# A macaron block of mixture-of-experts, linear attention and mixture-of-experts: rows of an expert pair merged by a TensorE product, and two output planes in place of four

## The chip, the cores and the metric

The kernel runs on one core of a Trainium2 chip. The metric is the device time of one execution in microseconds (us); the median of three is given. Five engines take part, each with an instruction queue of its own that is worked off strictly in order: TensorE (PE in the profile; its weight loads are PEld), VectorE (DVE), ScalarE (ACT), GpSimd (POOL) and SyncE (SP, which here only issues transfers). They meet through semaphores: an instruction can wait until a semaphore has reached a number, and everything behind it on its engine waits too.

## What is computed

The input is 8 sequences of 512 tokens of 128 features, so 4096 tokens. Three stages follow each other, each with a layernorm in front and its result added to `x`:

```python
x = x + 0.5 * ffn(layernorm(x))
x = x + linear_attention(layernorm(x))      # 16 heads of 8, causal
x = x + 0.5 * ffn(layernorm(x))

def ffn(x):                                  # E = 64 experts, K = 6, CAP = 64
    scores = softmax(x @ gate_w.T)
    _, idx = top_k(scores + gate_b, 6)       # weights are the unbiased scores
    # the first 64 (token, expert) pairs of an expert, in token order, get a slot
    h = silu(xb @ w1.T) * (xb @ w3.T)        # inner width 88
    yb = h @ w2.T
    y[token] += yb[expert, slot] * weight    # scatter-add over all slots
    z = silu(x @ ws1.T) * (x @ ws3.T) @ ws2.T    # shared expert, inner width 176
    return y + z
```

Both ffn stages use the same weights.

## The kernel before

Each ffn stage (`ffn(f)`, f = 0 and 1) has four parts.

**Routing.** Layernorm, logits, softmax and top 6 over four groups of 1024 tokens. Then the slot lists: `scan`, `differences`, `table`, `look_up` and `slots`, each in four quarters of 16 experts (`h` = 0 to 3), find for every slot its token. The quarters 0 and 1 are done ahead of the slab loop, 2 and 3 inside its first steps. `slots(h)` writes the row indices `tok_i` (for the gather) and `put_i` (for the scatter) of 8 slabs.

**The slab loop.** A slab is a pair of experts, 2 x 64 = 128 slots, one per partition; there are 32. Every engine writes its part as one loop over `s` with a software pipeline over three steps:

- POOL issues `gather(s)`, an indirect DMA (L466) that fetches 128 token rows into `GAT`, ten slabs ahead, and `add(s)` (L452), an indirect DMA that adds the 128 weighed rows `Y[:, s]` to the output planes in HBM. `add(s)` waits for `y_sb` of its slab. The scatter of slab `s` also waits until that of `s - 2` has landed.
- PE, in step `s`: `xb_turn(s)` (L758, a transpose), `hidden(s - 1)` (L769, four products), `expert_out(s - 2)` (L778, two products, the experts' output rows in PSUM), then `shared_part(s)`.
- ACT: `copy_xbT(s)`, `silu(s - 1)` and the silu of the shared layer (L560).
- DVE: `gate(s - 1)` (L1083), `weigh(s - 2)` (L1106 twice, PSUM to `Y`, times gate weight, times 0.5, signals `y_sb`), then its share of `shared_part(s)`.

**The shared expert** is spread over the same loop: for 8 groups of 512 tokens. Groups 6 and 7 have their first layer ahead of the loop. Groups 0 to 5 take four steps each from step 8 on (`s = 8 + 4g + k`): at k = 0 and 1 the first layer of one half (L705 on PE, two products of 512 columns; `shared_gate` on DVE, L1094), at k = 2 the second layer (`shared_out`, L718; `shared_add`, L1099), at k = 3 nothing.

**The output planes.** A token can be met by several slots, and two scatter-adds on one row of HBM must not race. So there are four planes, interleaved by token (`4 * token + plane`); the plane of a row is given by the half of the slab (which of the two experts) and by the slab's parity. The planes are zeroed ahead of use by SP (`clear_planes`, 2 MB each), and at the end of the ffn stage SP loads them back (L345) in four groups of 1024 tokens, into the tiles `A`, `PL`, `Bb` and `Cb`; DVE's `update(g)` adds the four planes of a group to `X` (L957, four instructions of 1024 elements per partition). In the middle of the program the next layernorm follows group by group (`stats` on DVE, `normalise` on ACT, L508); at the end the output store follows (L366).

The attention stage between the two is not touched.

What sets the order is the program text: each engine's instructions stand in the order in which its loop issues them. No scheduler moves them.

## Time and profile before

| | us |
|---|---|
| median of 3 runs (lowest, highest) | 533.45 (532.67, 536.54) |
| the profiled execution: its own time | 532.9 |
| the profiled execution: span, first to last instruction | 531.2 |
| PE, DVE, POOL, ACT busy in the span | 356.6, 307.6, 237.0, 207.8 |
| slab loop of f = 0: first gather to the last scatter's issue | 52.1 to 161.6 |
| slab loop of f = 1: the same | 393.3 to 497.0 |

The span is cut into stages that differ in what limits them, so the busy shares over the whole say little; the sections below go by stage. Times in rows are counted from the span's start. In the timeline a row has its start, its duration, the engine, the line and the operation, and in brackets how long the engine sat idle ahead of it and what ended that.

### The profile page before, as it was taken

Reading aid. Unit: us, or ns where it says so; the run is one execution under the profiler, and the core shown is the slowest. Engines: PE = TensorE matmul, PEld = TensorE weight load, DVE = VectorE, ACT = ScalarE, POOL = GpSimd, SP = SyncE. Lnnn points to the kernel's source line nnn. Section 1 sums busy time; section 2 is a strip of 40 time slices with the busy share of each in tenths; the row PEclk is TensorE's granted clock in tenths of the full one; section 3 lists DMA queues with packets and bytes.
Section 4 is the critical chain, followed back from the end, with each engine's and each line's share of the span. In section 5 each row is a group of like instructions: output and inputs, shape, how many; then the busy total and the mean of one; then the engine's idle time right before and its main releaser. Section 6 shows DMA issues by size and latency. Waiting matters only on the chain.

```text
span 531.2 us, 14693 instructions
## 1 busy us (share of the span) xinstructions
PE 356.6 (67%) x5808; PEld 263.3 (50%) x5812; DVE 307.6 (58%) x999; ACT 207.8 (39%) x543; POOL 237.0 (45%) x215
## 2 busy tenths in 40 slices
PE   0874589999960013598999999218848999998000
PEld 0851475666650012376788888118327667666000
DVE  6488363545430994454777775394985544545077
ACT  3983112322310067744677762169722232231000
POOL 7161747887872000403333333001537888887400
PEclk9987567999995556678999999657855699999555
DMA  8999961001015996000111111454200100100396
GB/s 272 369 268 341 318 185 15 5 11 14 5 6 218 407 401 239 2 2 2 40 40 40 40 40 49 109 218 139 61 8 8 12 11 6 17 5 6 108 426 257
DMA packets 49746, 62.64 MB, mean 118 GB/s; under 512 B 21701, under 2 KB 36248, under 8 KB 47183
## 3 DMA queue, kind: packets, MB, share of 16 engines
q1 hardware_dynamic: 37423, 60.51, 33.3%
q0 software_dynamic: 12288, 1.70, 3.2%
q8 instruction: 17, 0.28, 0.2%
q14 instruction: 18, 0.15, 0.1%
HBM read 39.53 MB, written 31.46 MB: 134 GB/s over the span
## 4 chain that ended last, share of the span: by engine, by line
PE 53%; DVE 23%; DMA 9%; ACT 6%; issue 5%; POOL 3%; SPq 1%; POOLq 0%; DVEq 0%; ACTq 0%
PE bank L769 6%; PE upper L864 5%; PE bank L705 5%; DVE X L957 5%; PE bank L718 5%; PE upper L705 4%; DMA Cb<-planes_d 4%; PE upper L778 3%; DVE Cb L1094 3%; DVE bn L962 3%; DVE Cb L1025 3%; POOL planes_d L452 3%; ACT Cb L560 2%; ACT A L508 2%; PE bank L880 2%
## 5 line engine op out<-in xcount | busy, mean ns | idle before, releaser
L452 POOL DMA_INDIRECT planes_d<-Bb,put_i x64 | 101.4, 1584 | 28.0 <-issue 14.8
L480 POOL TENSOR_TENSOR Bb<-Cb,chm 128x576 f32<-128x576 f32 x32 | 36.9, 1183 | 124.3 <-PE upper L909 69.6
L466 POOL DMA_INDIRECT A<-rows_d,tok_i x64 | 68.0, 1063 | 41.6 <-DVE put_i L1066 22.7
L672 PE MATMUL bank<-ident,A 128*128 128x128 f32 x96 | 21.3, 396 | 81.9 <-ACT A L508 65.1
L672 PEld LDWEIGHTS bank<-ident,A 128*128 128x128 f32 x96 | 17.0, 209 | 85.1 <-ACT A L508 52.3
L1106 DVE TENSOR_SCALAR Bb<-upper,A 64x128 f32<-64x128 f32 x128 | 44.4, 347 | 1.3
L1094 DVE TENSOR_TENSOR Cb<-Cb,upper 88x512 f32<-88x512 f32 x24 | 16.4, 683 | 44.8 <-ACT Cb L560 44.8
L769 PEld LDWEIGHTS bank<-ring,w1s 128*88 128x88 f32 x256 | 34.2, 191 | 8.0 <-issue 8.0
L433 POOL TENSOR_TENSOR Bb<-Eb,st 128x512 f32<-128x512 f32 x8 | 8.3, 1043 | 63.8 <-DVE st L1013 63.8
L560 ACT ACTIVATE Cb<-bank 88x512 f32<-88x512 f32 x24 | 14.2, 592 | 55.1 <-PE upper L705 55.1
L769 PE MATMUL bank<-ring,w3s 128*88 128x64 f32 x256 | 35.6, 270 | 0.0
L705 PE MATMUL bank<-XT,ws1s 128*88 128x512 f32 x56 | 32.1, 656 | 3.7 <-DVE Cb L1094 3.7
L769 PE MATMUL bank<-ring,w1s 128*88 128x64 f32 x256 | 34.1, 264 | 0.0
L1083 DVE TENSOR_TENSOR ring<-ring,bank 88x128 f32<-88x128 f32 x64 | 18.0, 281 | 26.2 <-ACT ring L572 26.1
L778 PE MATMUL upper<-w2s,ring 88*64 88x128 f32 x256 | 31.4, 328 | 0.1
L864 PE MATMUL upper<-A,Bb 32*32 32x128 f32 x1024 | 30.8, 273 | 1.0 <-issue 1.0
L769 PEld LDWEIGHTS bank<-ring,w3s 128*88 128x88 f32 x256 | 30.2, 185 | 0.0
L615 ACT ACTIVATE A<-Bb,hm 128x512 f32<-128x512 f32 x32 | 20.5, 711 | 24.1 <-PE upper L864 22.2
L705 PE MATMUL upper<-XT,ws3s 128*88 128x512 f32 x56 | 29.8, 615 | 0.0
L508 ACT ACTIVATE A<-X,st 128x128 f32<-128x128 f32 x72 | 28.6, 481 | 0.0
L957 DVE TENSOR_TENSOR X<-X,A 128x1024 f32<-128x1024 f32 x8 | 9.8, 1225 | 31.5 <-DMA A<-planes_d 31.3
L718 PE MATMUL bank<-ws2s,Cb 88*128 88x128 f32 x192 | 24.6, 281 | 3.9 <-DVE Cb L1094 3.6
(162 smaller groups left out, 804.7 us busy)
## 6 DMA issues: line engine op xcount, KB each, us to landing
planes_d<-zeros SPq DMA_DIRECT2D x8, 2048.0 KB, 15.9
rows_d<-A SPq DMA_DIRECT2D x8, 512.0 KB, 6.0
A<-planes_d SPq DMA_DIRECT2D x4, 1024.0 KB, 6.0
PL<-planes_d SPq DMA_DIRECT2D x4, 1024.0 KB, 10.0
Bb<-planes_d SPq DMA_DIRECT2D x4, 1024.0 KB, 13.7
Cb<-planes_d SPq DMA_DIRECT2D x4, 1024.0 KB, 18.0
w1s<-in_w1T SPq DMA_DIRECT2D x4, 704.0 KB
w3s<-in_w3T SPq DMA_DIRECT2D x4, 704.0 KB
```

Source lines behind the costliest of these rows:

```text
L452: pool.indirect_dma_start(out=planes_d[f], in_=Y[:, s, :], in_offset=None, out_offset=bass.IndirectOffsetOnAxis(ap=put_i[:, s:s + 1], axis=0),
L466: pool.indirect_dma_start(out=GAT[:, t % RING, :], out_offset=None, in_=rows_d, in_offset=bass.IndirectOffsetOnAxis(ap=tok_i[:, t:t + 1], ...
L480: pool.tensor_tensor(out=VX[:, :, :, c, :].rearrange("p q h f -> p (q h) f"), in0=VN.rearrange("p q h f -> p (q h) f"), in1=chm[:, c:c + 1 ...
L508: ins = act.activation(A[:, i, :], X[:, i, :], ACT.Identity, bias=st[:, 1, i:i + 1], scale=st[:, 4, i:i + 1])
L672: ins = pe.transpose(bank[g % 2][:, (i % 4) * P:(i % 4 + 1) * P], A[:, i, :], ident[:, :])
L705: ins = pe.matmul(bank[bk][0:I, :], w[:, k * I:(k + 1) * I], XT[:, 512 * g:512 * g + 512], start=True, stop=True)
L718: ins = pe.matmul(bank[SHARED[0]][:, i * D:(i + 1) * D], hs(g)[k][:, i * P:(i + 1) * P], ws2s[:, k, :], start=(k == 0), stop=(k == 1))
L769: ins = pe.matmul(bank[2 + s % 2][0:I, cols], w[:, 2 * s + k, :], XBT[s % 2][:, CAP * k:CAP * k + CAP], start=True, stop=True)
L778: ins = pe.matmul(bank[(4, 7)[s % 2]][CAP * k:CAP * k + CAP, 0:D], GT[s % 2][:, CAP * k:CAP * k + CAP], w2s[:, 2 * s + k, :], start=True, ...
L864: ins = pe.matmul(bank[4 + g][CHUNK * c:CHUNK * c + CHUNK, q * P:(q + 1) * P] .rearrange("p (j t) -> p j t", j=4), KT[rows, t0:t0 + CHUNK] ...
L957: then(dve.tensor_tensor(xt, xt, PLANES[g].rearrange("p (i k d) -> p i k d", i=GI, k=4)[:, :, k, :], ALU.add))
L1106: ins = dve.tensor_scalar(Y[rows, s, :], bank[(4, 7)[s % 2]][rows, 0:D], GAT[rows, s % RING, col:col + 1], 0.5, ALU.mult, ALU.mult)
```

## The change

Two output planes remain, one for each parity of the slab: the row is `2 * token + (s mod 2)`. So the two experts of a slab write to the same plane, and a token that both have would be met twice by one scatter. The kernel now merges such rows ahead of the scatter:

- `spread(h)` (DVE) writes for 8 slabs the token numbers of the first expert's 64 slots onto a diagonal (`ROWS`); `token_rows(h)` (PE, a product of ones with 512 columns) turns that into rows that hold those numbers on every partition; `match(h)` (DVE, four instructions) compares them with the second expert's token numbers, which gives 64x64 matrices `SAME` for 8 slabs, and moves the index of a second-half row that has a partner beyond the bounds, so that the scatter drops it.
- `merge(s)` (PE) multiplies `SAME` by the second half of `Y`, and `add_second(s)` (DVE) adds the product to the first half and signals `y_sb`.
- In each loop step PE issues `expert_out(s - 2)` ahead of `hidden(s - 1)`, and `merge(s - 2)` behind it. DVE issues `weigh(s - 2)` ahead of `gate(s - 1)`, and `add_second(s - 2)` behind it. `weigh` signals `weighed` and no longer halves; `update` does that (a multiply-add in place of an add).
- `table(3)` moves on DVE one step ahead, `look_up(3)` on PE one step back. The row turns stand at steps 0, 5, 11 and 19, `spread` ahead of the loop and at 4, 10 and 18, `match` at 1, 6, 11 and 19.
- The zeroing is 4 MB per ffn stage and all of it for f = 0 is issued at the start; the loads at the end of a stage are 4 MB in place of 8, and `update` has two instructions per group in place of four.

```diff
-        planes_d = [nc.dram_tensor(f"planes{f}_d", (4 * T, D), F32, kind="Internal").ap() for f in range(2)]
+        planes_d = [nc.dram_tensor(f"planes{f}_d", (2 * T, D), F32, kind="Internal").ap() for f in range(2)]
...
+        ROWS = Eb[0:CAP, :].rearrange("p (s c) -> p s c", s=NS)
+        SAME = Eb[CAP:P, :].rearrange("p (s c) -> p s c", s=NS)
...
-        PLANES = (A_flat, PL[:, :], Bb[:, 0:T], Cb[:, 0:T])
+        HP = T // 2
+        PLANES = (A_flat[:, 0:HP], A_flat[:, HP:T], PL[:, 0:HP], PL[:, HP:T])
...
-            clear_planes(sp, 0, (0, 1))
+            clear_planes(sp, 0)
...
-                    clear_planes(sp, 0, (2, 3))
                     for h in range(1, NQT):
                         load_experts(h)
...
+                def token_rows(h):
+                    pe.wait_ge(rows_set, NQT * f + h + 1)
+                    if NQT * f + h:
+                        pe.wait_ge(same_ready, NQT * f + h)
+                    ss = slice(QSL * h, QSL * h + QSL)
+                    pe.matmul(bank[LOOK[1]][CAP:P, :], ones[:, :], ROWS[:, ss, :].rearrange("p s c -> p (s c)"),
+                              start=True, stop=True).then_inc(rows_ps, 1)
+
+                def merge(s):
+                    if s % QSL == 0:
+                        pe.wait_ge(same_ready, NQT * f + s // QSL + 1)
+                    pe.wait_ge(weighed, f * NS + s + 1)
+                    pe.matmul(bank[(4, 7)[s % 2]][0:CAP, D:2 * D], SAME[:, s, :], Y[CAP:P, s, :], start=True, stop=True)\
+                        .then_inc(merged, 1)
...
                     if s < NS:
                         xb_turn(s)
+                    if s == 2:
+                        pe.wait_ge(dr_sb, NQT * (f + 1))
+                    if s == 3:
+                        pe.wait_ge(table_ready, NQT * (f + 1))
+                    if s >= 2:
+                        expert_out(s - 2)
                     if 1 <= s <= NS:
                         hidden(s - 1)
-                    if s == 2:
-                        pe.wait_ge(dr_sb, NQT * (f + 1))
                     if s >= 2:
-                        expert_out(s - 2)
+                        merge(s - 2)
+                    if s in ROW_TURN:
+                        token_rows(1 + ROW_TURN.index(s))
...
-                    for k in range(4):
-                        then(dve.tensor_tensor(xt, xt, PLANES[g].rearrange("p (i k d) -> p i k d", i=GI, k=4)[:, :, k, :], ALU.add))
+                    for k in range(2):
+                        then(dve.scalar_tensor_tensor(xt, PLANES[g].rearrange("p (i k d) -> p i k d", i=GI, k=2)[:, :, k, :], 0.5,
+                                                      xt, ALU.mult, ALU.add))
...
+                def spread(h):
+                    ss = slice(QSL * h, QSL * h + QSL)
+                    dve.tensor_tensor(ROWS[:, ss, :], ident[0:CAP, 0:CAP].unsqueeze(1).broadcast_to([CAP, QSL, CAP]),
+                                      sl[0:CAP, 1, ss].unsqueeze(2).broadcast_to([CAP, QSL, CAP]), ALU.mult).then_inc(rows_set, 1)
+
+                def match(h):
+
+                    ss = slice(QSL * h, QSL * h + QSL)
+                    dve.wait_ge(rows_ps, NQT * f + h + 1)
+                    then(dve.tensor_tensor(SAME[:, ss, :], bank[LOOK[1]][CAP:P, :].rearrange("p (s c) -> p s c", s=QSL),
+                                           sl[CAP:P, 1, ss].unsqueeze(2).broadcast_to([CAP, QSL, CAP]), ALU.is_equal))
+                    then(dve.tensor_reduce(sl[CAP:P, 0, ss], SAME[:, ss, :], AX, ALU.max))
+                    then(dve.scalar_tensor_tensor(sl[CAP:P, 0, ss], sl[CAP:P, 0, ss], float(T), sl[CAP:P, 1, ss], ALU.mult, ALU.add))
+                    dve.scalar_tensor_tensor(put_i[CAP:P, ss], sl[CAP:P, 0, ss], 2.0, plane0[CAP:P, ss], ALU.mult, ALU.add)\
+                        .then_inc(same_ready, 1)
...
-                        ins = dve.tensor_scalar(Y[rows, s, :], bank[(4, 7)[s % 2]][rows, 0:D], GAT[rows, s % RING, col:col + 1], 0.5,
-                                                ALU.mult, ALU.mult)
-                    ins.then_inc(y_sb, 1)
+                        ins = dve.tensor_scalar(Y[rows, s, :], bank[(4, 7)[s % 2]][rows, 0:D], GAT[rows, s % RING, col:col + 1], None,
+                                                ALU.mult)
+                    ins.then_inc(weighed, 1)
+
+                def add_second(s):
+                    dve.wait_ge(merged, f * NS + s + 1)
+                    dve.tensor_tensor(Y[0:CAP, s, :], bank[(4, 7)[s % 2]][0:CAP, D:2 * D], Y[0:CAP, s, :], ALU.add).then_inc(y_sb, 1)
 
                 for s in range(NS + 2):
+                    if s >= 2:
+                        weigh(s - 2)
                     if 1 <= s <= NS:
                         gate(s - 1)
+                    if s == 1:
+                        match(0)
                     if s >= 2:
-                        weigh(s - 2)
+                        add_second(s - 2)
                     if s == 1:
                         slots(2)
-                    elif s == 2:
                         table(3)
                     elif s == 3:
                         slots(3)
+                    elif s in SPREAD:
+                        spread(1 + SPREAD.index(s))
+                    elif s in MATCH:
+                        match(1 + MATCH.index(s))
```

How the order on PE changes in the steady part of the loop, from the shared first layer of k = 1 to the second layer of k = 2. Before, `xb_turn` (L758), `hidden` (L769), `expert_out` (L778), then the next shared layer (L718):

```order
L705 MATMUL bank<-XT,ws1s 88x512 [waits sh_gated]
L705 MATMUL upper<-XT,ws3s 88x512
L758 MATMUL bank<-ident,A 128x128 [waits xbT_sb,gathered2]
L769 MATMUL bank<-ring,w1s 88x64 [waits gated,xbT_sb]
L769 MATMUL bank<-ring,w1s 88x64
L769 MATMUL bank<-ring,w3s 88x64 x2
L778 MATMUL upper<-w2s,ring 64x128 [waits y_sb,gated]
L778 MATMUL upper<-w2s,ring 64x128
L718 MATMUL bank<-ws2s,Cb 128x128 [waits sh_gated,tokens_ready]
L718 MATMUL bank<-ws2s,Cb 128x128 x7
```

The same step in the changed kernel (L718 is the shared first layer, L773 the transpose, L808 `expert_out`, L784 `hidden`, L800 `merge`, L731 the second layer):

```order
L718 MATMUL bank<-XT,ws1s 88x512 [waits sh_gated]
L718 MATMUL upper<-XT,ws3s 88x512
L773 MATMUL bank<-ident,A 128x128 [waits xbT_sb,gathered2]
L808 MATMUL upper<-w2s,ring 64x128 [waits y_sb,gated]
L808 MATMUL upper<-w2s,ring 64x128
L784 MATMUL bank<-ring,w1s 88x64 [waits gated,xbT_sb]
L784 MATMUL bank<-ring,w1s 88x64
L784 MATMUL bank<-ring,w3s 88x64 x2
L800 MATMUL upper<-Bb,Eb 64x128 [waits weighed,same_ready]
L731 MATMUL bank<-ws2s,Cb 128x128 [waits sh_gated,tokens_ready]
L731 MATMUL bank<-ws2s,Cb 128x128 x7
```

`expert_out` went ahead of `hidden`, and a product that waits for `weighed` now stands between `hidden` and the next shared layer.

On DVE, the same steps before: L1094 is the shared gate, L1083 `gate`, L1106 `weigh`.

```order
L1094 TENSOR_TENSOR Cb<-Cb,upper 88x512 [waits sh_silu]
L1083 TENSOR_TENSOR ring<-ring,bank 88x128 [waits y_ps,silu_done]
L1106 TENSOR_SCALAR Bb<-upper,A 64x128 [waits y_ps]
L1106 TENSOR_SCALAR Bb<-upper,A 64x128
L1094 TENSOR_TENSOR Cb<-Cb,upper 88x512 [waits sh_silu]
L1083 TENSOR_TENSOR ring<-ring,bank 88x128 [waits y_ps,silu_done]
L1106 TENSOR_SCALAR Bb<-upper,A 64x128 [waits y_ps]
L1106 TENSOR_SCALAR Bb<-upper,A 64x128
```

In the changed kernel (L1149 shared gate, L1161 `weigh`, L1138 `gate`, L1167 `add_second`):

```order
L1149 TENSOR_TENSOR Cb<-Cb,upper 88x512 [waits sh_silu]
L1161 TENSOR_SCALAR Bb<-upper,A 64x128 [waits y_ps]
L1161 TENSOR_SCALAR Bb<-upper,A 64x128
L1138 TENSOR_TENSOR ring<-ring,bank 88x128 [waits y_ps,silu_done]
L1167 TENSOR_TENSOR Bb<-upper,Bb 64x128 [waits merged]
L1149 TENSOR_TENSOR Cb<-Cb,upper 88x512 [waits sh_silu]
L1161 TENSOR_SCALAR Bb<-upper,A 64x128 [waits y_ps]
L1161 TENSOR_SCALAR Bb<-upper,A 64x128
L1138 TENSOR_TENSOR ring<-ring,bank 88x128 [waits y_ps,silu_done]
L1167 TENSOR_TENSOR Bb<-upper,Bb 64x128 [waits merged]
```

`weigh` now stands directly behind the shared gate of the step before, and `add_second` waits for PE. The third place is DVE in step 1 and at the first `weigh`; before: `gate(0)`, `slots(2)` (L1062 to L1066), `gate(1)`, `weigh(0)`.

```order
L1083 TENSOR_TENSOR ring<-ring,bank 88x128 [waits silu_done]
L1062 TENSOR_SCALAR top<-bank,c_of_p 128x256 [waits look_ps]
L1063 TENSOR_REDUCE sl<-top 128x8 [waits dve_step]
L1064 TENSOR_TENSOR sl<-sl,bank 128x8 [waits dve_step]
L1065 CAST tok_i<-sl 128x8 [waits dve_step]
L1066 SCALAR_TENSOR_TENSOR put_i<-sl,plane 128x8
L1083 TENSOR_TENSOR ring<-ring,bank 88x128 [waits silu_done]
L1106 TENSOR_SCALAR Bb<-upper,A 64x128 [waits y_ps]
L1106 TENSOR_SCALAR Bb<-upper,A 64x128
```

In the changed kernel `match(0)` (L1116 to L1120), `slots(2)` (L1100 to L1104) and `table(3)` (L1091, L1092) stand in a row:

```order
L1138 TENSOR_TENSOR ring<-ring,bank 88x128 [waits silu_done]
L1116 TENSOR_TENSOR Eb<-upper,sl 64x512 [waits rows_ps]
L1118 TENSOR_REDUCE sl<-Eb 64x8 [waits dve_step]
L1119 SCALAR_TENSOR_TENSOR sl<-sl 64x8 [waits dve_step]
L1120 SCALAR_TENSOR_TENSOR put_i<-sl,plane 64x8 [waits dve_step]
L1100 TENSOR_SCALAR top<-bank,c_of_p 128x256 [waits look_ps]
L1101 TENSOR_REDUCE sl<-top 128x8 [waits dve_step]
L1102 TENSOR_TENSOR sl<-sl,bank 128x8 [waits dve_step]
L1103 CAST tok_i<-sl 128x8 [waits dve_step]
L1104 SCALAR_TENSOR_TENSOR put_i<-sl,plane 64x8
L1091 TENSOR_SCALAR lo_b<-upper 128x16 [waits lo_ps]
L1092 TENSOR_TENSOR Bb<-slot_ce,lo_b 128x1024 [waits dve_step]
```

Behind that piece come the two halves of `weigh(0)`; `match(0)` is new there and `table(3)` came from behind `weigh(0)`.

## Rows read from the trace of the kernel before

**Rows 1.** The page, clock that the throttle granted TensorE, tenths, 40 slices.

```profile
PEclk9987567999995556678999999657855699999555
```

**Rows 2.** Timeline of POOL: last scatter of f = 0, then f = 1.

```profile
161.58 1.55 POOL L452 DMA_INDIRECT planes_d<-Bb,put_i  x1 [0.30 <-issue]
...
407.51 1.63 POOL L452 DMA_INDIRECT planes_d<-Bb,put_i  x1 [0.30 <-issue]
...
450.28 1.59 POOL L452 DMA_INDIRECT planes_d<-Bb,put_i  x1 [0.31 <-issue]
...
453.53 1.59 POOL L452 DMA_INDIRECT planes_d<-Bb,put_i  x1 [0.31 <-DMA planes_d<-Bb,put_i]
...
497.00 1.55 POOL L452 DMA_INDIRECT planes_d<-Bb,put_i  x1 [0.31 <-issue]
```

**Rows 3.** Timeline, 104 to 116 us: one turn of four slabs, f = 0.

```profile
104.00 0.27 PE L758 MATMUL upper<-ident,A 128*128 128x128 f32 x1
...
108.19 0.27 PE L758 MATMUL upper<-ident,A 128*128 128x128 f32 x1
...
108.39 0.59 ACT L560 ACTIVATE Cb<-bank 88x512 f32<-88x512 f32 x1 [1.98 <-PE upper L705]
...
109.02 0.68 DVE L1094 TENSOR_TENSOR Cb<-Cb,upper 88x512 f32<-88x512 f32 x1 [1.66 <-ACT Cb L560]
...
109.76 1.09 PE L705 MATMUL bank<-XT,ws1s 128*88 128x512 f32 x2 [0.32 <-DVE Cb L1094]
...
109.82 0.71 DVE L1106 TENSOR_SCALAR Bb<-upper,A 64x128 f32<-64x128 f32 x2
...
115.00 0.27 PE L758 MATMUL upper<-ident,A 128*128 128x128 f32 x1
...
115.20 0.69 DVE L1099 SCALAR_TENSOR_TENSOR X<-bank,X 128x512 f32<-128x512 f32 x1 [1.32 <-PE bank L718]
```

**Rows 4.** The chain that ended last (start, us, what): PE ahead of the shared layers.

```profile
82.64 1.94 PE bank L705 x2
...
410.97 1.13 PE bank L769 x8
...
413.15 1.13 PE bank L769 x8
...
419.34 1.86 PE bank L705 x2
```

**Rows 5.** Timeline, first and last steps of both loops, PE and DVE.

```profile
59.16 0.47 PE L758 MATMUL bank<-ident,A 128*128 128x128 f32 x1 [4.93 <-DMA A<-rows_d,tok_i]
...
153.01 0.70 DVE L1106 TENSOR_SCALAR Bb<-upper,A 64x128 f32<-64x128 f32 x2
...
395.63 0.45 PE L758 MATMUL bank<-ident,A 128*128 128x128 f32 x1 [0.16 <-DMA A<-rows_d,tok_i]
...
404.33 0.69 DVE L1054 TENSOR_TENSOR Bb<-slot_ce,lo_b 128x1024 bf16<-128x1024 bf16 x1
...
409.19 0.48 DVE L1062 TENSOR_SCALAR top<-upper,c_of_p 128x256 f32<-128x256 f32 x1
...
410.44 0.16 DVE L1066 SCALAR_TENSOR_TENSOR put_i<-sl,plane 128x8 int32<-128x8 f32 x1
...
488.73 0.70 DVE L1106 TENSOR_SCALAR Bb<-upper,A 64x128 f32<-64x128 f32 x2
```

**Rows 6.** Groups by line: a DVE reduction over 512 columns.

```profile
L1007 DVE TENSOR_REDUCE st<-bank 128x8 f32<-128x512 f32 x4 | 2.8, 692 | 9.6 <-PE bank L679 9.6
```

**Rows 7.** Chain and timeline, behind the slab loops: loads, updates, layernorm.

```profile
164.73 6.93 DMA A<-planes_d
...
179.03 4.97 DVE L957 TENSOR_TENSOR X<-X,PL 128x1024 f32<-128x1024 f32 x4
...
194.24 3.19 ACT L508 ACTIVATE A<-X,st 128x128 f32<-128x128 f32 x8
...
523.01 5.00 DVE L957 TENSOR_TENSOR X<-X,Cb 128x1024 f32<-128x1024 f32 x4 [0.36 <-DMA Cb<-planes_d]
```

More of the change, by code:

```diff
@@ L67, in macaron_kernel @@
     EARLY = 2
+    SPREAD, ROW_TURN, MATCH = (4, 10, 18), (5, 11, 19), (6, 11, 19)
     QS = float(E) ** -0.5
@@ L222, in macaron_kernel @@
         y_sb = sem("y_sb")
+        rows_set = sem("rows_set")
+        rows_ps = sem("rows_ps")
+        same_ready = sem("same_ready")
+        weighed = sem("weighed")
+        merged = sem("merged")
         added = [sem(f"added{k}") for k in range(2)]
@@ L289, in macaron_kernel, with clear_planes @@
         block = ctx.enter_context(nc.Block())
-        def clear_planes(queue, f, parts=range(4)):
-            for k in parts:
+        def clear_planes(queue, f):
+            for k in range(2):
                 dst = planes_d[f][k * T:(k + 1) * T, :].rearrange("(p a i) d -> p a (i d)", p=P, i=4)
@@ L422, in _ @@
                 count(c_of_p[k * CAP:(k + 1) * CAP, :], 0, [[0, 1]], 1)
-                count(plane0[k * CAP:(k + 1) * CAP, :], k, [[0, NS // 2], [2, 2]], 0)
+                count(plane0[k * CAP:(k + 1) * CAP, :], 0, [[0, NS // 2], [1, 2]], 0)
+            then(pool.memset(ones[:, :], 1.0))
             pool.iota(slot_ce[:, :, :], pattern=[[1, CAP], [0, NE]], base=0, channel_multiplier=0,
@@ L793, in ffn @@
                         look_up(2)
+                        token_rows(0)
                     elif s == 1:
                         differences(3)
-                    elif s == 2:
+                    elif s == 3:
                         look_up(3)
@@ L955, in update @@
                     dve.wait_ge(part_in[g], 16 + 32 * (1 + n // 2))
-                    for k in range(4):
-                        then(dve.tensor_tensor(xt, xt, PLANES[g].rearrange("p (i k d) -> p i k d", i=GI, k=4)[:, :, k, :], ALU.add))
+                    for k in range(2):
+                        then(dve.scalar_tensor_tensor(xt, PLANES[g].rearrange("p (i k d) -> p i k d", i=GI, k=2)[:, :, k, :], 0.5,
+                                                      xt, ALU.mult, ALU.add))
                     dve.memset(st[:, 0, 0:1], 0.0).then_inc(group_ready, 1)
@@ L1065, in slots @@
                     dve.tensor_copy(tok_i[:, ss], sl[:, 1, ss])
-                    dve.scalar_tensor_tensor(put_i[:, ss], sl[:, 1, ss], 4.0, plane0[:, ss], ALU.mult, ALU.add)\
+                    dve.scalar_tensor_tensor(put_i[0:CAP, ss], sl[0:CAP, 1, ss], 2.0, plane0[0:CAP, ss], ALU.mult, ALU.add)\
                         .then_inc(tokens_ready, 1)
+                def spread(h):
[11 more added lines that the diff above has]
+                        .then_inc(same_ready, 1)
                 scan(0)
@@ L1076, in ffn @@
                 slots(1)
+                spread(0)
                 table(2)
```

15 lines of the change are left out of this document (9 added, 6 removed).

## The prediction

> **What bounds the kernel now.** I read the views from the coarse to the fine: the page, POOL's timeline over both slab loops, then PE and DVE inside one turn of four slabs, the first steps of the loop, and what follows the loop.
>
> The slab loop is set by POOL. In its steady part one scatter and one gather take 3.25 us per slab (450.28 to 453.53), with only 0.3 us of idle time ahead of each [rows 2]. PE needs less: a turn of four slabs with the shared expert's three parts takes 11.0 us (104.00 to 115.00), 2.75 per slab [rows 3]. So PE and DVE are done early: the last `weigh` of f = 1 ends at 489.43 [rows 5], but the last scatter is issued only at 497.00 [rows 2]. For f = 0 it is 153.71 against 161.58. PE thus has 7.6 to 7.9 us to give per loop, and in the steady part 0.5 us per slab. Whatever it loses beyond that is paid in full.
>
> Behind the loop the planes bound: their first group lands 6.9 us after the start of the load, DVE then spends 5.0 us per group on the four additions, and at the very end it does nothing else until 528 [rows 7].
>
> **Gains behind the loops.** The first group is 1 MB in place of 2. In f = 1 the 8 MB and some 1.5 MB of output beside them took from about 2.8 us behind the last scatter's issue [rows 2] to 523.0, where DVE had waited a moment for the last group [rows 7]: 9.5 MB in 23.2 us, 0.41 MB/us. So the first group comes 2.5 us earlier. An `update` of 1024 elements takes 1.24 us (4.97 / 4) [rows 7]; the multiply-add should cost the same, since a multiply-add and a multiplication of 512 columns take 0.69 and 0.68 [rows 3]. Two fewer in each of four groups are 4 x 2.5 = 10.0 us.
> - f = 0: ACT needs 3.2 us per group for `normalise` [rows 7] and more for its copies. DVE's group shrinks from 7.5 to 5.0, so ACT becomes nearly as slow as DVE; I take 9.4 of the 10.0. With the load: -12.0 (bounds -9 and -13).
> - f = 1: DVE works off four groups in 10 us, but the last group only lands about (4 + 1) MB / 0.41 = 12.2 us after the load's issue at 499.8. Then 2.5 for its update and the 3.1 us that now lie between the last update and the end of the span (528.0 and 531.2): 517.6, with 1 us for the latency of the load 518.7. That is -12.5 (bounds -10 and -13.5).
>
> The smaller zeroing (4 MB less, with the expert weights behind it on SP's queue) helps the start of f = 0: PE's first transpose there waited 4.93 us for its gather, and 0.16 in f = 1 [rows 5]. I take 2 us of it (bounds 0 and 4.5). The rest of the zeroing lies beside other work.
>
> **The steady part of the loop.** What is added on PE is one product of 128 columns per slab. It is not in the trace; the nearest row is the transpose with 128 columns, 0.27 us [rows 3]. If that were all, a turn would take 11.0 + 1.1 = 12.1 us, still under POOL's 13.0, and it would be free. But `merge` waits for `weigh`, and PE takes nothing out of turn. Follow the rows of the step at 108.19 [rows 3]. ACT's silu of the shared layer starts at 108.39, DVE's shared gate runs from 109.02 to 109.70, and PE's next shared layer starts at 109.76, after 0.32 of waiting for that gate. In the changed order `weigh` stands behind that same gate: 109.70 + 0.71 = 110.41. Then comes `merge`, 0.27, so the next shared layer starts at 110.73, **0.97 later**. The step from k = 1 to k = 2 is the same. In step k = 3 `shared_add` (115.20 to 115.89) holds DVE [rows 3]: `weigh` to 116.60, `merge` to 116.92, where a bare step ends about 1.2 after 115.00 (2.18 at half clock, 410.97 to 413.15 [rows 4], of which not quite all halves): +0.75. In step k = 0 DVE is free; `weigh` ends together with `hidden`, which leaves the product and a semaphore: +0.35 to 0.4. A turn becomes 11.0 + 2 x 0.97 + 0.75 + 0.4 = **14.1 us, above POOL's 13.0**. The bound passes from POOL to the ring of PE, ACT and DVE. Six turns: +18.6 on PE's own time line.
>
> At steps 11 and 19 `token_rows` and `match` come on top. `token_rows` has 512 columns, as each of the shared layer's two products, which takes 1.09 us with its tail [rows 3] and holds PE for 0.93 (half of 1.86 at half clock [rows 4]). `match` has a comparison and a reduction over 512 columns (0.68 and 0.69 [rows 3, 6]) and two small steps: 1.8. DVE is late with the next `weigh` by about 1.4. Together 2.3 each: +4.6. At the end `weigh(31)` stands behind `shared_add` and is followed by `merge` and `add_second`: +1.25. So from step 8 to the last `y_sb` the changed loop needs 24.5 us more than PE and DVE need now.
>
> **The start of the loop.** It runs at half clock: five to six tenths from 385 to 425 and full after that [rows 1]. PE goes from its first transpose at 395.63 [rows 5] to the first shared layer at 419.34 [rows 4] in 23.7 us. Walking the new order from 395.63 at these durations:
> - `spread(0)` (0.7) delays `table(2)`, and `token_rows(0)` takes 1.86 at half clock [rows 4]. `hidden(0)` ends at 403.0, `gate(0)` at 403.6.
> - DVE then does `match(0)` (1.8), `slots(2)` (1.4, as 409.19 to 410.60) and `table(3)` (0.9, its long part 0.69) ahead of `weigh(0)` [rows 5], so `weigh(0)` ends at 408.5 and `merge(0)` at 409.0. PE is at step 3 at 409.0 in place of 406.2.
> - `look_up(3)` and `slots(3)` with two early shared gates (1.3) hold `weigh(2)`: step 5 starts at 416.7 in place of 410.5.
> - `spread(1)`, two more gates, then `token_rows(1)` (1.86): step 6 at 422.2 in place of 412.7. `match(1)` and two more merges at 0.45: the first shared layer at 431.1.
>
> That is **+11.7 us** (bounds: 0, if DVE's work hides; 13, if every piece adds up). The last `y_sb` of f = 1 is then at 489.43 + 11.7 + 24.5 = 525.6, and the last scatter moves from 497.0 to 525.7: **+28.7**. For f = 0 the same from 59.16 - 2: first shared layer at 92.6 in place of 82.6 [rows 4], last `y_sb` 153.71 + 9.7 + 24.5 = 187.9, and with a little slack 188.2 against 161.58: **+26.6**.
>
> **The sum.** Against the profiled execution's own 532.9 us (span 531.2): -12.0 - 12.5 + 26.6 + 28.7 = +30.8, which gives 563.7. The median of the runs shown is 0.55 above that execution: **564 us**.
>
> **The clock.** Through both steady parts the granted clock stayed at nine tenths or more [rows 1], that is, at its 2.4 GHz level. The changed order puts a wait of 1.0 us ahead of three of four merges, where now there is 0.3. The Trainium skill (TensorE: Matmul & The Clock Gate, section "A second HAM failure mode: psum-queue depth-cycling") says that short idle times between groups of products can make the clock swing between its two levels. That speaks against this change; that PE already waits briefly twice in each turn and keeps its clock shows only that so much is borne. Its price goes by rows, below.
>
> **Rivals.**
> 1. *The merge is hidden* (faster). `weigh` would have to end ahead of `hidden` in every step. Then a turn is 12.1 us, POOL stays the bound, and only its first scatters start 2 or 3 us late: the first was issued at 407.51 [rows 2]. 532.9 - 24.5 + 3 = 511. It decides at a turn of 13.0 us. For it: the product is short, DVE is idle half of the loop. Against it: the written order on DVE and the ends of the rows at 109.70 and 109.76.
> 2. *The start hides its work, the steady part does not.* Without the 11.7 and 9.7: 543. Something between is likelier than all of it: 541 to 551.
> 3. *The clock falls in the loop.* Where it does, each of the shared layer's two products holds PE for 1.86 in place of 0.93 [rows 4] and a bare step takes 2.18 in place of 1.2: about 2.8 us per fall. At the four places with `match`: +11, so 576; in all twelve turns: +34, so 598.
>
> **How the numbers follow.** Forecast (552 to 575): 0.62. Rival 1: 0.08. Rival 2: 0.15. Rival 3: 0.12. The remaining 0.03 is a time within 1% of now, which is also about what a measurement of this kernel tells from no change. The range goes from rival 2's foot to the lower foot of rival 3: 543 to 580. Faster by over 1%: 0.08; within 1%: 0.03; slower: 0.89.
>
> **What would show it.** In the steady part PE's `merge` is released by DVE's `weigh`, with about 1 us of idle time at k = 1 and 2, and four slabs take about 14.1 us. POOL's scatters wait for `add_second`, and its busy share in the loop falls. The first shared layer of f = 1 starts 35 us after the first transpose, not 24. The last scatter's issue comes within 0.1 us of the last `add_second`. `update` takes 2.5 us per group. I am wrong if POOL still runs with 0.3 us gaps through the steady part, if `weigh` ends ahead of `hidden`, or if the clock drops between 100 and 180 us.

## The result, and the profile after

The changed kernel takes **574.3 us** (568.15 to 577.75, 4 runs), the one before 533.06 (532.35 to 536.54, 4 runs): ratio 1.0721, 95% interval 1.0609 to 1.0834. The ratio leaves out the longest run, 577.75, which was over 1.5% above the fastest. The profiled execution took 576.4 us with a span of 574.7, 43.5 more than before. The four executions lie 10 us apart, and the two shorter ones have the higher mean granted clock (0.819 and 0.814, against 0.799 and 0.801).

Where the 43.5 us are, counted in both traces between the same events:

| stretch | before | after | difference | forecast |
|---|---|---|---|---|
| start to the last scatter's issue, f = 0 | 161.58 | 199.63 | +38.05 | +26.6 |
| behind it, to the end of ACT's last `normalise` (L508, now L520) | 43.3 | 31.5 | -11.8 | -12.0 |
| middle, to the first gather of f = 1 | 188.4 | 186.7 | -1.7 | 0 |
| first gather to last scatter, f = 1 | 103.7 | 135.0 | +31.3 | +28.7 |
| behind it | 34.2 | 21.9 | -12.3 | -12.5 |

The timeline of the changed kernel in f = 1, where two shared first layers (L718) are one step apart (start, duration, engine, line, operation, and in brackets the idle time ahead with what ended it). It answers to [rows 3].

```profile
473.72 0.43 PE L800 MATMUL upper<-Bb,Eb 64*64 64x128 f32 x2 [1.25 <-DVE Bb L1161]
474.08 1.09 PE L718 MATMUL bank<-XT,ws1s 128*88 128x512 f32 x2
...
476.69 0.68 DVE L1149 TENSOR_TENSOR Cb<-Cb,upper 88x512 f32<-88x512 f32 x1 [2.23 <-ACT Cb L572]
...
477.30 0.71 DVE L1161 TENSOR_SCALAR Bb<-upper,A 64x128 f32<-64x128 f32 x2
...
478.06 0.43 PE L800 MATMUL upper<-Bb,Eb 64*64 64x128 f32 x2 [0.78 <-DVE Bb L1161]
...
478.42 1.09 PE L718 MATMUL bank<-XT,ws1s 128*88 128x512 f32 x2
478.53 0.28 DVE L1167 TENSOR_TENSOR Bb<-upper,Bb 64x128 f32<-64x128 f32 x1 [0.21 <-PE upper L800]
...
479.61 1.59 POOL L464 DMA_INDIRECT planes_d<-Bb,put_i  x1 [1.40 <-DVE Bb L1167]
...
488.45 1.09 PE L718 MATMUL bank<-XT,ws1s 128*88 128x512 f32 x2
```

PE has finished `hidden` and stands 0.78 us in front of `merge` (L800), because `weigh` (L1161) only starts when the shared gate (L1149) is through. The next shared layer starts 0.36 us behind the merge's start. POOL's scatter is released by `add_second` (L1167) after 1.40 us of idle time, where before there were 0.3. A turn of four slabs takes 488.45 - 474.08 = 14.37 us. The list of waits (total us, times, longest) says the same of both loops:

```profile
POOL planes_d L464 <- DVE Bb L1167: 81.6, 42, 9.1
...
PE upper L800 <- DVE Bb L1161: 34.1, 49, 2.0
```

POOL used to set the loop and waited 9.3 us in all for DVE's rows; it now waits 81.6. The last scatter too is released by `add_second`, 0.76 us behind its end in f = 1 (552.08 to 552.84), and behind the loop `update` (L994) has two instructions per group:

```profile
199.63 1.55 POOL L464 DMA_INDIRECT planes_d<-Bb,put_i  x1 [4.10 <-DVE Bb L1167]
...
551.80 0.28 DVE L1167 TENSOR_TENSOR Bb<-upper,Bb 64x128 f32<-64x128 f32 x1 [0.52 <-PE upper L800]
...
552.84 1.55 POOL L464 DMA_INDIRECT planes_d<-Bb,put_i  x1 [1.93 <-DVE Bb L1167]
```

```profile
560.75 2.49 DVE L994 SCALAR_TENSOR_TENSOR X<-A,X 128x1024 f32<-128x1024 f32 x2 [6.28 <-DMA A<-planes_d]
...
568.98 2.48 DVE L994 SCALAR_TENSOR_TENSOR X<-PL,X 128x1024 f32<-128x1024 f32 x2 [0.42 <-DMA PL<-planes_d]
```

That is 2.49 us where [rows 7] have 5.0.

The two loops differ by their start and by the clock. The first transposes of f = 0 and of f = 1 and the first merge of f = 1 (PE's timeline):

```profile
60.84 0.48 PE L773 MATMUL bank<-ident,A 128*128 128x128 f32 x1 [6.29 <-DMA A<-rows_d,tok_i]
...
420.18 0.45 PE L773 MATMUL bank<-ident,A 128*128 128x128 f32 x1 [0.17 <-DMA A<-rows_d,tok_i]
...
433.16 0.66 PE L800 MATMUL upper<-Bb,Eb 64*64 64x128 f32 x2 [2.01 <-DVE Bb L1161]
```

In the chain that ended last, the first shared layer of f = 1 follows at 456.44, 36.3 us behind its first transpose; in f = 0 it is 96.28, 35.4 behind. The clock by stretches of f = 0 (busy time and count of PE, PEld, DVE, ACT, POOL, then the granted clock as a share of 2.4 GHz, DMA share, GB/s):

```profile
100.00:108.00 8.00, 6.71 (x43) 4.25 (x43) 4.33 (x11) 2.02 (x6) 3.28 (x4) 0.93 0.05 8
108.00:120.00 12.00, 11.68 (x45) 6.47 (x44) 5.00 (x13) 1.10 (x4) 6.75 (x5) 0.50 0.02 1
120.00:136.00 16.00, 14.40 (x95) 8.44 (x94) 6.83 (x20) 3.85 (x12) 9.05 (x8) 0.96 0.05 5
...
192.00:200.00 8.00, 7.13 (x36) 5.87 (x35) 2.44 (x7) 1.56 (x2) 3.47 (x3) 0.56 0.02 2
```

For 12 us in the middle of the loop, and from 193 on at its end, PE ran at the 1.2 GHz level. From the first transpose to the last scatter f = 0 took 138.8 us, f = 1, which kept the full clock from 460 on, 132.7. From the first shared layer on it is 103.4 against 96.4.

### The profile page after: what moved, and what is told of

It reads as the page before. It is cut to its first block, busy times and chain, and to the rows that moved or that the text cites. A ratio compares the mean times of both kernels' runs of the same rounds, so it can differ in the third digit from the quotient of the medians.

```text
span 574.7 us, 15085 instructions
## 1 busy us (share of the span) xinstructions
PE 415.0 (72%) x5952; PEld 282.3 (49%) x5956; DVE 327.2 (57%) x1087; ACT 208.9 (36%) x543; POOL 237.5 (41%) x216
## 4 chain that ended last, share of the span: by engine, by line
PE 52%; DVE 27%; ACT 7%; issue 7%; DMA 6%; SPq 1%; POOLq 0%; DVEq 0%; ACTq 0%
DVE Bb L1161 6%; PE bank L731 6%; PE upper L800 5%; PE upper L901 5%; PE bank L718 5%; PE upper L718 4%; ACT A L520 3%; ACT Cb L572 3%; PE bank L784 2%; DVE Cb L1063 2%; DVE bn L1000 2%; PE bank L858 2%; PE bank L917 2%; PE bank L684 2%; PE bank L691 2%
## 5 line engine op out<-in xcount | busy, mean ns | idle before, releaser
L464 POOL DMA_INDIRECT planes_d<-Bb,put_i x64 | 101.6, 1588 | 96.6 <-DVE Bb L1167 81.6
L684 PE MATMUL bank<-ident,A 128*128 128x128 f32 x96 | 21.7, 401 | 61.2 <-ACT A L520 49.5
L800 PE MATMUL upper<-Bb,Eb 64*64 64x128 f32 x128 | 31.6, 333 | 34.5 <-DVE Bb L1161 34.1
L1161 DVE TENSOR_SCALAR Bb<-upper,A 64x128 f32<-64x128 f32 x128 | 44.4, 347 | 11.2 <-PE upper L808 10.1
L1149 DVE TENSOR_TENSOR Cb<-Cb,upper 88x512 f32<-88x512 f32 x24 | 16.4, 683 | 58.1 <-ACT Cb L572 58.1
L584 ACT ACTIVATE ring<-bank 88x128 f32<-88x128 f32 x64 | 17.5, 273 | 62.4 <-PE bank L784 62.4
L784 PE MATMUL bank<-ring,w1s 128*88 128x64 f32 x256 | 39.3, 285 | 0.0
L784 PEld LDWEIGHTS bank<-ring,w1s 128*88 128x88 f32 x256 | 30.1, 185 | 13.3 <-issue 8.7
L784 PE MATMUL bank<-ring,w3s 128*88 128x64 f32 x256 | 36.2, 274 | 0.0
L800 PEld LDWEIGHTS upper<-Bb,Eb 64*64 64x64 f32 x128 | 13.7, 150 | 43.8 <-DVE Bb L1161 32.9
L808 PE MATMUL upper<-w2s,ring 88*64 88x128 f32 x256 | 32.8, 341 | 1.1 <-ACT A L562 0.9
L718 PE MATMUL bank<-XT,ws1s 128*88 128x512 f32 x56 | 33.0, 674 | 0.0
L1138 DVE TENSOR_TENSOR ring<-ring,bank 88x128 f32<-88x128 f32 x64 | 18.1, 283 | 23.8 <-ACT ring L584 22.6
L718 PE MATMUL upper<-XT,ws3s 128*88 128x512 f32 x56 | 31.3, 643 | 0.0
L784 PEld LDWEIGHTS bank<-ring,w3s 128*88 128x88 f32 x256 | 30.8, 189 | 0.0
L578 ACT ACTIVATE ring<-upper 128x128 f32<-128x128 f32 x32 | 8.7, 272 | 56.1 <-PE upper L773 56.1
```

Source lines behind the costliest of these rows:

```text
L464: pool.indirect_dma_start(out=planes_d[f], in_=Y[:, s, :], in_offset=None, out_offset=bass.IndirectOffsetOnAxis(ap=put_i[:, s:s + 1], axis=0),
L684: ins = pe.transpose(bank[g % 2][:, (i % 4) * P:(i % 4 + 1) * P], A[:, i, :], ident[:, :])
L718: ins = pe.matmul(bank[bk][0:I, :], w[:, k * I:(k + 1) * I], XT[:, 512 * g:512 * g + 512], start=True, stop=True)
L784: ins = pe.matmul(bank[2 + s % 2][0:I, cols], w[:, 2 * s + k, :], XBT[s % 2][:, CAP * k:CAP * k + CAP], start=True, stop=True)
L800: pe.matmul(bank[(4, 7)[s % 2]][0:CAP, D:2 * D], SAME[:, s, :], Y[CAP:P, s, :], start=True, stop=True)\
L808: ins = pe.matmul(bank[(4, 7)[s % 2]][CAP * k:CAP * k + CAP, 0:D], GT[s % 2][:, CAP * k:CAP * k + CAP], w2s[:, 2 * s + k, :], start=True, ...
```

## The experiments

Ratios are to the kernel before, run on the same chip in the same job; they compare runs of different jobs better than the medians do. "Plane kernels" (e1, e2, e8, e9) have the two output planes and drop the second half of each slab's rows at the scatter, so part of the result is missing from their output.

| run | what it is | median us | ratio, interval | profiled span |
|---|---|---|---|---|
| e1_planes_only | two planes, loop as before | 511.15 | 0.9554, 0.9506 to 0.9602 | 506.3 |
| e9_no_merge_new_order | e1 with the new order in a step | 512.82 | 0.961, 0.9526 to 0.9694 | 510.0 |
| e2_no_match | e9 with merge and its waits | 548.41 | 1.0226, 1.018 to 1.0272 | 546.3 |
| (the change) | and with the matching | 574.3 | 1.0721, 1.0609 to 1.0834 | 574.7 |
| e3_merge_free | the change, PE not waiting for `weigh` | 537.32 | 1.0037, 1.0003 to 1.0071 | 534.5 |
| e4_merge_late | the change, merge one step later | 540.18 | 1.0081, 1.0052 to 1.011 | 536.5 |
| e5_early_match | the change, other start | 570.37 | 1.0666, 1.0572 to 1.0759 | 565.4 |
| e6_late_early | e4 and e5 | 532.68 | 0.997, 0.9939 to 1.0 | 532.9 |
| e7_late_early_loads | e6, weight loads held back | 530.7 | 0.9925, 0.9893 to 0.9957 | 532.8 |
| e8_planes_only_loads | e1, weight loads held back | 512.04 | 0.9566, 0.9523 to 0.9608 | 511.0 |
| e10_old_order | e6 with the old order in a step | 553.64 | 1.0337, 1.0262 to 1.0411 | 552.4 |
| e11_old_order_quarters | e10, half of the loads held back | 552.33 | 1.0307, 1.0226 to 1.0388 | 552.0 |
| e12_quarters | e6, half of the loads held back | 529.39 | 0.9928, 0.9898 to 0.9958 | 528.5 |

**e1, the planes alone.** No `spread`, `token_rows`, `match`, `merge` or `add_second`; `weigh` signals `y_sb`; second-half indices out of bounds; both loops in the old order.

```diff
-                    ins.then_inc(weighed, 1)
+                    ins.then_inc(y_sb, 1)
+            dve.memset(put_i[CAP:P, :], 4 * T)
```

> Two planes, half the zeroing and loads, two additions per group, and nothing of the merge: no row turns, no matching, no product, loop order as before. The second expert's rows are left out of the result (their indices lie beyond the bounds). Theory A (the gains lie behind the loops and the loss is all in the loop): 24 us are gained, 509 us. Rival (part of the gain is only paid back elsewhere, by the attention stage or by transfers that now collide): above 515.

511.15, 24 us less by its ratio and as expected: this is the gain behind the loops with nothing to pay for it. The last scatters are where they were (161.38; in f = 1 103.9 us behind the first gather against 103.7).

**e2, merge without matching.** The changed kernel with `merge` and its waits, but zeros as its left operand, and no row turns.

```diff
-                    pe.matmul(bank[(4, 7)[s % 2]][0:CAP, D:2 * D], SAME[:, s, :], Y[CAP:P, s, :], start=True, stop=True)\
+                    pe.matmul(bank[(4, 7)[s % 2]][0:CAP, D:2 * D], zeros[CAP:P, 0:CAP], Y[CAP:P, s, :], start=True, stop=True)\
```

> The changed kernel without spread, token_rows and match; merge, add_second and their waits stay, with a matrix of zeros as the weights of the product. The second expert's rows are left out of the result. Theory A (the wait of PE for weigh costs 3.4 us per turn of four slabs, matching costs the start of the loop and two steps): the turn stays at 14.4 us, the first shared layer comes 5 us later than before instead of 12 to 15, 547 us. Rival B (matching is the main cost, DVE would keep up without it): the turn is 12.5 us, POOL is the bound again, 515 us. Rival C (the granted clock is the main cost): falls back to full clock everywhere, 560 us or more if it still drops.

548.41. The steady turn is the same as in the changed kernel: two merges a turn apart, both after 0.78 us of waiting, stand 14.37 us apart.

```profile
465.73 0.43 PE L795 MATMUL upper<-Bb,zeros 64*64 64x128 f32 x2 [0.78 <-DVE Bb L1155]
...
470.07 0.43 PE L795 MATMUL upper<-Bb,zeros 64*64 64x128 f32 x2 [0.79 <-DVE Bb L1155]
...
480.10 0.43 PE L795 MATMUL upper<-Bb,zeros 64*64 64x128 f32 x2 [0.78 <-DVE Bb L1155]
```

**e3, merge without the wait.** The full matching, but the product takes zeros in place of `Y` and writes to another bank, so that PE needn't wait for `weigh`; the partner rows are not added. The cut also has two waits that keep the sums in order (`hidden` for `y_sb`, `add_second` for `weighed`).

```diff
-                    pe.wait_ge(weighed, f * NS + s + 1)
-                    pe.matmul(bank[(4, 7)[s % 2]][0:CAP, D:2 * D], SAME[:, s, :], Y[CAP:P, s, :], start=True, stop=True)\
+                    pe.matmul(bank[2 + s % 2][0:CAP, 2 * D:3 * D], SAME[:, s, :], zeros[CAP:P, 0:D], start=True, stop=True)\
```

**e4, the merge one step later.** The whole computation: `merge(s - 3)` stands behind the transpose of step `s`, `add_second(s - 3)` behind `gate`.

```diff
                         xb_turn(s)
+                    if s >= 3:
+                        merge(s - 3)
...
-                    if s >= 2:
-                        merge(s - 2)
```

> The changed kernel with the product at the same place and of the same size, but on zeros and into another bank, so that it needs no weigh: PE does all the work and does not wait. Left out of the result: the rows that would be merged. Row turns and matching stay. Theory A (it is the wait, not the work): the turn is about 12.5 us on PE, below POOL's 13.0, and only the start stays late: 535 to 545 us. Rival B (PE's work and DVE's busy time cost by themselves): the turn stays over 14 us, 565 us or more.

> The full computation. merge(s - 3) stands at the start of step s behind the transpose, one step later than in the change, and add_second with it; nothing else differs. Theory A: weigh has ended a step earlier, PE no longer waits for it, turn of 12.5 us or POOL's 13.0, start as late as in the changed kernel: 535 to 545 us. Rival (the wait only moves to add_second or to the next product in PSUM): 560 us or more.

537.32 and 540.18. Two different ways of taking the wait from PE, one that leaves the sum out and one that keeps it, give back 34 to 37 us (in the profiled execution, 7 of them are the clock's, see below). The same place as above, in e3:

```profile
444.85 1.06 PE L718 MATMUL bank<-XT,ws1s 128*88 128x512 f32 x2 [0.23 <-DVE put_i L1120]
...
447.95 0.43 PE L800 MATMUL bank<-zeros,Eb 64*64 64x128 f32 x2
448.31 1.09 PE L718 MATMUL bank<-XT,ws1s 128*88 128x512 f32 x2
...
457.28 1.09 PE L718 MATMUL bank<-XT,ws1s 128*88 128x512 f32 x2
```

The product costs PE 0.36 us, and the turn takes 12.43, below POOL's 13.0. With the wait it was 14.37: 1.94 us per turn were waiting. In e4 PE's merge still waits four times, 3.8 us in all, at the start of the loops; in the change it was 34.1 us in 49 waits. No stretch of the steady part fell to the lower clock in e2, e3, e4 or e6.

**e5, e6, the other start.** `spread(0)` right behind `slots(0)`, `token_rows(0)` ahead of `look_up(1)`, `match(0)` ahead of the loop, `slots(2)` and the early shared gates one or more steps later. e6 adds the late merge.

```diff
+                token_rows(0, 2)
+                look_up(1)
...
-                    if s == 1:
-                        match(0)
...
-                    if s in (3, 4):
+                    if s in (5, 7):
```

> The changed kernel with another start only, full computation: spread(0) directly behind slots(0), token_rows(0) ahead of look_up(1) where PE is idle and into another bank, match(0) behind table(2) where DVE is idle, slots(2) one step later, the early shared gates at steps 5 and 7. merge stays where the change put it. Theory A (in the start, DVE's and PE's matching work stands ahead of the first weigh at half clock, and that costs 6 to 8 us per loop apart from the waits of the steady part): 560 us, turn still 14.4 us. Rival (the late start is made up later, since POOL or PE has slack): 572 us or more.

> Full computation: merge one step later (as in the fourth run) and the other start (as in the fifth) together. Theory A (the two losses are separate and add up): 528 us, a little faster than the kernel before; turn 13.0 us, POOL's. Rival (with the wait gone, the start is hidden already): 538 us or more.

e5 is a **miss**: 570.37, 4 us gained and not 14. The start did get shorter (in f = 0 30.2 us from the first transpose to the first shared layer against 35.4; the first scatter of f = 1 comes 14.3 us behind the first gather against 17.1). But in the profiled execution #41 to #64 of the scatters took 88.6 us against 85.2, and PE's clock fell there. It fell at all four places with matching in the steady parts, each time at a merge that waited 1.25 us (111.14, 142.95, 460.91 and 493.71); at the last one the shared layer behind it ran slowly:

```profile
493.71 0.43 PE L804 MATMUL upper<-Bb,Eb 64*64 64x128 f32 x2 [1.25 <-DVE Bb L1165]
494.07 1.60 PE L718 MATMUL bank<-XT,ws1s 128*88 128x512 f32 x2
```

Its four runs go from 565 to 575 us, with clocks of 0.812 to 0.785, so by medians and by ratios (2.9 us) its gain is not clear of the noise. e6 takes 532.68, between the expected 528 and the rival's 538: 7.5 less than e4 by medians, 5.9 by ratios.

**e7, e8, the loads.** After the change the first gather of f = 0 still landed late. SP now waits for it before it sends the expert weights of quarters 1 to 3.

```diff
+                    sp.wait_ge(gathered[0], 16)
                     for h in range(1, NQT):
                         load_experts(h)
```

> The same, and SP holds the expert weights of the quarters 1 to 3 back until the first gather of the first stage has landed. Theory A on the gather (it is the weight loads that make the first gather take 8 us in the first stage against 2 to 3 in the second, not the zeroing that the change took away): the first transpose of f = 0 comes 4 to 5 us earlier, 524 us. Rival (the zeroing at the start still delays it): no difference in the first transpose.

> The kernel of the first run (two planes, no merge, the second expert's rows left out of the result) with the same holding back of the weight loads. Theory A: 3 to 4 us less than the first run, 507 us, since POOL's first scatters waited 4.3 us in f = 0. Rival: 511 us.

The first transpose came at 55.62 in e7 and at 62.94 in e6. Part of this is that the gather was issued at 52.12 and 54.37; counted from there it landed after 3.5 us and 8.6, so it was the weight loads that delayed it. But the times are **misses**, 530.7 and 512.04 where 524 and 507 were expected; the first is 2 us below e6, the second no shorter than e1. The DMA engines are now full up to the first scatter at 71.36 and two thirds busy for 8 us behind it (e7, columns as above), and a scatter waits for the landing of the one two before it:

```profile
60.00:64.00 4.00, 1.14 (x6) 0.46 (x6) 1.06 (x3) 0.87 (x2) 3.09 (x4) 0.50 1.04 293
64.00:68.00 4.00, 3.64 (x20) 2.43 (x20) 1.50 (x5) 0.77 (x3) 1.81 (x2) 0.50 1.01 279
68.00:72.00 4.00, 4.00 (x35) 3.05 (x31) 2.91 (x12) 0.55 (x2) 0.64 (x1) 0.50 1.00 295
```

```profile
81.67 1.59 POOL L465 DMA_INDIRECT planes_d<-Bb,put_i  x1 [3.36 <-DMA planes_d<-Bb,put_i]
```

**e9, the order alone.** e1 with `expert_out` ahead of `hidden` on PE and `weigh` ahead of `gate` on DVE (not shown), and with `table(3)` and `look_up(3)` where the change has them.

```diff
-                    if 1 <= s <= NS:
-                        hidden(s - 1)
                     if s >= 2:
                         expert_out(s - 2)
+                    if 1 <= s <= NS:
+                        hidden(s - 1)
```

> Part of the change: two planes as in e1 (no merge, no match, the second half's rows dropped, so that part of the result is left out), but with the new order inside each step: on PE expert_out ahead of hidden, on DVE weigh ahead of gate. It prices the order by itself. Theory A (what costs is the merge and PE's wait ahead of it): the order is nearly free, the loop stays POOL's (turn 13.0 us), and only the bare steps at half clock lose some tenths each: 511 to 515 us, against 511.2 of e1. Theory B (the new order already lengthens the ring of PE and DVE beyond POOL's 3.25 us per slab): 520 us or more.

512.82, as expected: by its ratio 3 us more than e1, with intervals that overlap. In the steady part PE's turn is 11.7 us in place of 11.0 (the shared layers at 113.23 and 124.91), which POOL's 13.0 still covers. At half clock the price is larger. Two transposes that follow each other in e9's bare steps, f = 1:

```profile
404.38 0.42 PE L770 MATMUL bank<-ident,A 128*128 128x128 f32 x1
...
405.26 0.69 PE L803 MATMUL upper<-w2s,ring 88*64 88x128 f32 x4 [0.47 <-DVE ring L1130]
...
407.12 0.42 PE L770 MATMUL upper<-ident,A 128*128 128x128 f32 x1
```

2.74 us, and 2.17 in e1 (402.16 to 404.33). `expert_out` (L803) now needs the gate of the `hidden` that went just ahead of it, and only the transpose covers that round over ACT and DVE. With the merge in between, a bare step takes 3.01 (e2, 422.33 to 425.34).

**e10, the old order with the late merge.** Against e6:

```diff
-                    if 2 <= s < NS + 2:
-                        expert_out(s - 2)
                     if 1 <= s <= NS:
                         hidden(s - 1)
+                    if 2 <= s < NS + 2:
+                        expert_out(s - 2)
...
-                    if 2 <= s < NS + 2:
-                        weigh(s - 2)
-                    if 1 <= s <= NS:
-                        gate(s - 1)
                     if s >= 3:
                         add_second(s - 3)
+                    if 1 <= s <= NS:
+                        gate(s - 1)
+                    if 2 <= s < NS + 2:
+                        weigh(s - 2)
```

> The whole computation, with the merge one step later and the first match ahead of the loop as in e6, but in each step PE does hidden, then expert_out, and DVE does add_second, gate, then weigh: the order inside a step that the kernel before has. Theory A: hidden's weights and columns no longer wait for expert_out, so the gate starts sooner and the steps at half clock at the start get 0.2 us shorter each, eight of them per loop; the steady part keeps POOL's pace: 526 to 530 us, against 532.7 of e6. Rival (add_second as the first thing on DVE makes the gate late, or the order plays no part): 532 to 537 us.

A **miss of both sides**: 553.64, 21 us slower than e6. With `weigh` last in DVE's step the late merge has to wait after all, at the bare step between two shared groups, and everything behind it too. PE in e10, f = 1:

```profile
488.95 0.33 PE L783 MATMUL bank<-ident,A 128*128 128x128 f32 x1
489.96 0.43 PE L804 MATMUL upper<-Bb,Eb 64*64 64x128 f32 x2 [0.68 <-DVE Bb L1165]
...
491.95 2.01 PE L718 MATMUL bank<-XT,ws1s 128*88 128x512 f32 x2
...
498.31 0.27 PE L783 MATMUL bank<-ident,A 128*128 128x128 f32 x1
...
511.38 0.27 PE L783 MATMUL bank<-ident,A 128*128 128x128 f32 x1
```

A turn takes 511.38 - 498.31 = 13.07 us, where e6 has 12.33 (481.27 to 493.60), so PE is no faster than POOL and makes up nothing of what the start costs. And the clock fell behind this wait: the shared layer's first product holds PE for 1.80 us (491.95 to 493.75) in place of 0.93. The same happened behind two such waits in f = 0 (at 120.97 and 162.34), but not behind the one at 504.61.

**e11, e12, half of the loads.** As e10 and e6, but quarter 1 is sent at once and only 2 and 3 wait.

```diff
                     for h in range(1, NQT):
+                        if h == 2:
+                            sp.wait_ge(gathered[0], 16)
                         load_experts(h)
```

> As e10, and SP holds back only the expert weights of the quarters 2 and 3 until the first gather has landed, where e7 held back 1, 2 and 3. If the loads that follow collide with the first scatters less when quarter 1 is already in, the first gather lands 2 to 3 us sooner and less of it is paid back at the first scatters: 2 us less than e10, so 524 to 528. If what delays the first gather is the load of quarter 1 alone, it lands after 7 us or more and the time is that of e10 within 1 us.

> The whole computation: e6 with the expert weights of the quarters 2 and 3 held back until the first gather has landed, quarter 1 sent at once (in e7 all three were held back). e11 against e10 showed that this lets the first gather land as early as in e7. If the collision with the first scatters comes from the volume that is still under way then, a third less of it costs less: 1 to 2 us below e7's 530.7, so 529, ratio 0.985 to 0.99. If the pay-back is in the loop's later part whatever is loaded (in e11 2.8 us at the first scatter had become 0.5 at the last), it is 530 to 532, as e7.

In e11 the first transpose came at 57.19 against e10's 62.42, in e12 at 57.59: 3.2 us after the gather's issue in both. e11 was no faster than e10 (552.33), so its 524 to 528, which rested on e10's expectation, is a miss too. e12, the best version of the whole computation, takes 529.39 (12 runs, 528.19 to 538.05), ratio 0.9928: 0.7% faster than the kernel before, and not to be told from e7.

## Why the prediction came out as it did

The forecast said slower, by a ring of PE and DVE in the place of POOL, and gave 564 with a range of 543 to 580. 574.3 lies in it, 10 us above the forecast; the profiled execution's 576.4 is already outside the 552 to 575 that were called the forecast. The range's upper end, 580, isn't worked out anywhere: rival 3 at four places is 564 + 11 = 575, not 576.

- **Behind the loops**: -12.0 and -12.5 forecast, -11.8 and -12.3 measured. e1 shows the same alone: -24 us by its ratio.
- **The steady turn**: 14.1 forecast, 14.37 measured, with the step from k = 1 to 2 taking 4.34 (forecast 3.35 + 0.97 = 4.32). The mechanism is shown by e3 and e4 from two sides. The product was mis-sized: 0.36 us, where I had taken 0.27 from the transpose. It is an f32 product in two instructions, and the transpose behind which I had priced it is one. So even unhindered a turn is 12.43, not 12.1. Four products at 0.09 too little are 0.36 per turn, which covers the surplus of 0.27, or 1.6 us per loop.
- **The match steps**: 2.3 forecast, and 16.35 - 14.37 = 1.98 measured (488.45 to 504.80).
- **The last scatter** was to come within 0.1 us of the end of the last `add_second`. It came 0.76 behind, in both loops.
- **The start**: 35.4 us forecast, 35.4 and 36.3 measured. The sum was nearly right but not all its parts: a merge in a bare step was priced at 0.45, while order and merge together cost 3.01 - 2.17 = 0.84 at half clock. e9 separates them: 0.57 for the order, which I had costed at nothing, and 0.27 more with the merge. The transposes of f = 1 show where the walk went. Counted from the first, step 3 came at 13.6 us (forecast 13.4), step 5 at 21.7 (21.1) and step 6 at 26.5 (26.6), so the step with `token_rows(1)` was 0.65 too dear; from there to the first shared layer it was 9.7 in place of 8.9. Rival 2, that the start hides, is out.
- **The gather relief in f = 0** is one of the two steps that failed. I let the first transpose come 2 us earlier, at 57.2, because half of the zeroing was gone. It came at 60.84, so +3.7, and 8.4 us after its issue where it had been 7.1. e7, e8, e11 and e12 show that the weight loads hold the gather up. With less zeroing ahead of them they were only issued sooner (the last at 44.87 in place of 53.09) and still met the gather: from 52 to 56 us the DMA engines were as full as before (1.04 and 1.01).
- **The clock** is the other. The forecast kept it, with a fall as rival 3, and named a fall between 100 and 180 us as a sign that it was wrong. That sign came: in f = 0 it fell at 108 for 12 us, behind a merge that had waited 0.88 us (106.39), and again at 193. Between the same rows of the two loops the first fall cost 4.6 us and the second 1.9; with 0.4 at the clock's rise they make the 7.0 by which f = 0 took longer from the first shared layer on. This is a partial rival 3: not the 11 us at the four places with matching (two in each loop), and f = 1 has none. The Trainium skill (TensorE: Matmul & The Clock Gate, section "A second HAM failure mode: psum-queue depth-cycling") says that short waits between groups of products can make the clock swing. The runs agree so far as falls in the steady part came in kernels whose merge waits for `weigh` (the change, e5, e10 and e11), and none in e3, e4 and e6. But e2 has the same 0.78 us waits and kept its clock, and in f = 1 of the changed kernel so did a wait of 1.25 us ahead of 474. That the waits are the cause is therefore likely but not shown, and which wait tips it is not settled.

Together: 3.7 (gather) + 7.0 (clock) + 2.6 (the rest from the first shared layer to the last scatter, both loops, mostly the turn) + 0.8 (start, f = 1) + 0.4 (behind the loops) - 1.7 (middle) = 12.8, against the 12.7 us by which the profiled span exceeds the forecast of 562.0. So gather and clock make up most of the miss in size; that the time still fell in the range owes something to its width.

Where the time goes, by ratios: the planes give -24 us, the order +3 (within the noise), the merge with its wait +33, the matching +26. And where the planes' gain goes in e12, by its profiled span, 2.7 us below that of before: the stretch from the last scatter of f = 0 to the first gather of f = 1 is 16.0 us shorter and the end 12.5, but from the first gather to the last scatter the loops take 119.0 and 117.7 us where before there were 109.5 and 103.7, +23.5, and the first gather was issued 2.3 us later. The start at half clock takes longer, and PE's turn is 12.33 us (e6) in place of 11.0, so its lead of 7.6 to 7.9 us over POOL is gone: from the 9th to the last scatter f = 1 takes 70.8 us and not 63.0.

## What to carry to other kernels

A small product that needs another engine's result costs what its engine waits, not what it takes: here 0.36 us of work came with 0.78 of waiting, and with the same product one step later PE's waits for it fell from 34.1 us to 3.8, and the program took 34 us less. Before adding such a hop, count the slack of the engine that isn't the bound (here 0.5 us per slab and 7.6 in all); once a turn passes the old bound, every step pays. And a change of order that is free by itself (e9) can be what keeps another wait hidden (e6 against e10): reorder and re-time both engines of a hop together.
